# Second buffers, new PSUM banks, 96+96 contraction and a new order behind the experts of a five-stage transformer kernel

## The chip, the cores and the metric

The kernel runs on one core of one Trainium2 chip. The metric is the device time of one execution in microseconds; 2% of it is 7.3 us. One launch does all of the work, from the images to the output.

## The reference

Sixteen inputs of 96 tokens (64 image patches and 32 text rows), each token 192 wide, in float32:

```
h = tok(x);  h = concat([h, txt], axis=1)                 # 16 x 96 x 192
h = h + attn0(layernorm(h));  h = h + experts(layernorm(h))
# the part that is changed:
q, k, v = layernorm(h) @ w_qkv.T                          # 12 heads of 16
q = q / max(sum_n |q|, 1e-12);  k = k / max(sum_n |k|, 1e-12)
h = h + (q @ (k^T v)) @ w_proj.T + b_proj                 # linear attention
Xn = l2_normalize(layernorm(h));  sp = l2_normalize(slots) * scale
logits = Xn @ sp                                          # 96 tokens x 32 slots
D = softmax(logits, over tokens);  C = softmax(logits, over slots)
H = gelu((D^T Xn) @ W_down + b_down);  h = h + C @ (H @ W_up + b_up)
```

## The kernel before, in words

The 16 inputs are four groups `j` of four. A group has 384 tokens, held as `NB = 3` blocks of 128 rows; a block holds 32 tokens of each of its four inputs. `h[:, j, blk]` is the running sum. Each engine (TensorE `pe`, ScalarE `act`, VectorE `ve`, GpSimd `gp`, SyncE `sp`) has one program, written out by hand as a list of calls, and carries it out strictly in that order. Engines meet only at semaphores. `free(name=count)` in TensorE's list is a wait that protects a PSUM bank or a buffer; `need(...)` is one inside a helper.

The tokens, the first attention and the experts take the first 260 us and are not changed. Behind them TensorE first does `combine(j, part)`: the experts' rows of groups 0 and 1 are weighed and added into `h`; groups 2 and 3 get theirs by indirect DMAs that GpSimd issues (`fetch_row`) and VectorE adds (`add_rows`). Then comes, for each group, one round of the linear attention:

- VectorE `linear_moments`, GpSimd `norm_scale("b", ...)`, VectorE `linear_norm`: the layer norm, into `xn`.
- TensorE `turn_linear`: turns `xn` into PSUM; ScalarE `keep_linear_inputs` copies it to `xnT`.
- TensorE `linear_queries` and `linear_keys_values`; ScalarE copies to `q1T` and `kv1`. The 192 features are contracted as 128 + 64. `xnT[:, 0]` holds features 0 to 127; `xnT[:, 1]` holds the other 64 twice, in rows 0 to 63 and 64 to 127, so that two matmuls of 64 rows can run side by side in the two halves of the array.
- TensorE `key_products` (k^T v, L801) and `key_sums` (sum of |k|, L809; VectorE `key_norms` makes `abs_k` for it).
- VectorE `own_heads` masks the products into `kv_bd`; `query_norms`, `norm_products` and `scale_queries` scale `q1T`.
- TensorE `linear_outputs` (L820), ScalarE `keep_linear_outputs` to `o1T`, TensorE `linear_project` in two parts (L830), VectorE `add_linear`.

And one round of the soft mixture: VectorE `soft_moments`, GpSimd `soft_scale`, VectorE `soft_norm` into `xs`; TensorE `turn_soft`, ScalarE `keep_soft_inputs` to `xsT`; TensorE `soft_logits` (L850); VectorE `soft_max`, `token_shift`; ScalarE `exp_slots`, `exp_tokens`; VectorE `slot_weights` into `dsp_bd` and `token_weights`; TensorE `soft_inputs` (L858), ScalarE `keep_slots`. For all groups together: `soft_hidden` (groups 0 to 2, then 3, L866), `gelu_slots`, `keep_own`, then for each group `slot_outputs` (L873), `add_up_bias`, `token_outputs` (L882), `add_soft` and the stores.

The buffers `xn`, `o1T`, `xs`, `xsT`, `dsp_bd` and the small statistics exist once, so that for instance `linear_norm(j)` needs `turn_linear(j - 1)` to be over. PSUM has eight banks: 0 and 1 serve the turned inputs and the queries, 2 to 4 the keys and values, 1 to 4 the key products, 1 and 2 the outputs, 3 and 4 the projection, 5 to 7 the soft mixture. A copy out of a bank must be over before the next user writes it.

## Time and profile before

| | |
|---|---|
| time, median of 3 runs | 366.97 us (364.63 to 372.05) |
| the profiled execution | 366.12 us, its span 364.0 us |
| TensorE busy | 325.9 us, 90% of the span |
| VectorE / ScalarE / GpSimd busy | 195.5 / 112.1 / 52.1 us |
| first combine matmul | 259.81 us |
| end of the last matmul | 360.13 us |

The table is read so: TensorE is busy nine tenths of the time, but that is a mean over the program. In the 40 slices of the page it stands at 9 or more up to about 260 us and lower behind it. All that is changed lies between 259.81 and 360.13 us, 100.3 us long; behind it come one addition by VectorE and the last stores, 3.9 us. A TensorE duration in the rows includes the emptying of its pipeline; where steps follow one another without a wait, the step's price is from its start to the start of the next. The 9 to 48 instructions of one step stand in one row; a float32 matmul counts as two instructions.

### The profile page before, as it was taken

What the parts mean: (1) busy time and instruction counts of PE and PEld (TensorE: products, weight loads), DVE (VectorE), ACT (ScalarE), POOL (GpSimd) and SP (SyncE); (2) the same over time, 40 slices, a digit from 0 to 9 for tenths busy, and PEclk for the clock granted to TensorE, in tenths of its full rate; (3) what the DMA queues carried; (4) which work ended last, traced back from release to release, by engine and by line L of the source; (5) the groups of instructions that cost most, each with busy time, mean ns of one, the idle gap of its engine ahead of it and who ended that gap; (6) DMA issues with size and microseconds to landing.
All of it is one profiled execution on the core that took longest, in us unless ns stands there. A gap on an engine that the chain in (4) does not pass through costs nothing.

```text
span 364.0 us, 9315 instructions
## 1 busy us (share of the span) xinstructions
PE 325.9 (90%) x3978; PEld 216.6 (60%) x3978; DVE 195.5 (54%) x636; ACT 112.1 (31%) x218; POOL 52.1 (14%) x99
## 2 busy tenths in 40 slices
PE   4898999887788989999999999999987899997765
PEld 3675567655665337475656657475854556666455
DVE  2925497899999971142312111120367655968655
ACT  1224444665642431404041221203012213333140
POOL 8403222100011000000010000000087201100100
PEclk9999999999999999999999999999999989999889
DMA  7936011332030000504132240000012000000005
GB/s 266 346 85 220 2 38 31 117 125 96 19 105 1 2 0 2 151 17 137 50 103 74 81 137 16 23 2 22 24 54 67 13 0 0 3 2 2 0 0 130
DMA packets 15876, 23.29 MB, mean 64 GB/s; under 512 B 3770, under 2 KB 11932, under 8 KB 15836
## 3 DMA queue, kind: packets, MB, share of 16 engines
q1 hardware_dynamic: 14364, 20.93, 18.4%
q0 software_dynamic: 576, 1.18, 1.2%
q10 hardware_dynamic: 896, 0.59, 0.7%
q8 instruction: 31, 0.51, 0.6%
q14 instruction: 9, 0.07, 0.1%
HBM read 19.94 MB, written 2.75 MB: 62 GB/s over the span
## 4 chain that ended last, share of the span: by engine, by line
PE 61%; DVE 20%; SPq 7%; issue 4%; DMA 3%; POOL 2%; ACT 2%; DVEq 0%; POOLq 0%; ACTq 0%
PE banks L719 18%; PE banks L734 17%; SPq L320 4%; PE banks L496 3%; PE banks L249 3%; PE banks L778 2%; PE banks L858 2%; DVE sb_onehot_combT L1695 2%; PE banks L820 2%; PE banks L830 2%; PE banks L788 2%; DMA sb_tok_xeT<-in_xhalo 2%; DVE sb_stat L1517 1%; POOL sb_onehot_combT L455 1%; PE banks L782 1%
## 5 line engine op out<-in xcount | busy, mean ns | idle before, releaser
L719 PE MATMUL banks<-sb_tok_xeT,sb_wi_sl 128*128 128x480 f32 (+1 forms) x192 | 64.9, 590 | 1.1 <-ACT sb_tok_xeT L1236 1.1
L734 PE MATMUL banks<-sb_wo_sl,sb_attn_hidT_attn 128*60 128x192 f32 x768 | 64.1, 327 | 0.0
L734 PEld LDWEIGHTS banks<-sb_wo_sl,sb_attn_hidT_attn 128*60 128x60 f32 x768 | 52.9, 133 | 12.4 <-issue 4.0
L1251 ACT ACTIVATE sb_attn_hidT_attn<-banks 128x480 f32<-128x480 f32 x48 | 25.6, 569 | 95.7 <-PE banks L719 95.7
L719 PEld LDWEIGHTS banks<-sb_tok_xeT,sb_wi_sl 128*128 128x128 f32 (+1 forms) x192 | 24.9, 187 | 37.7 <-issue 35.8
L1743 DVE COPY sb_w_tok_e_out<-banks 60x384 f32<-60x384 f32 x16 | 8.9, 555 | 61.9 <-PE banks L734 61.6
L496 PE MATMUL banks<-sb_tok_xeT 128*32 128x193 f32 (+1 forms) x512 | 24.7, 328 | 1.5 <-DMA sb_tok_xeT<-in_xhalo 1.5
L496 PEld LDWEIGHTS banks<-sb_tok_xeT 128*32 128x32 f32 (+1 forms) x512 | 17.2, 109 | 7.2 <-issue 4.5
L1745 DVE COPY sb_onehot_combT<-banks 60x384 f32<-60x384 f32 x16 | 8.9, 555 | 22.1 <-PE banks L734 22.0
L618 PE MATMUL banks<-sb_w_v,sb_xrT 97*32 97x96 f32 x512 | 13.7, 249 | 1.8 <-issue 1.2
L1155 ACT ACTIVATE sb_onehot_combT<-sb_tok_xeT 128x1024 f32<-128x1024 f32 x8 | 8.5, 1058 | 19.3 <-DMA sb_tok_xeT<-in_xhalo 19.0
L1517 DVE BATCH_NORM_STATS2 sb_stat<-sb_h 128x6 f32<-128x192 f32 x48 | 14.1, 348 | 0.5
L858 PE MATMUL banks<-sb_attn_hidT_attn 128*96 128x128 f32 x48 | 8.8, 353 | 5.7 <-DVE sb_attn_hidT_attn L1865 5.7
L618 PEld LDWEIGHTS banks<-sb_w_v,sb_xrT 97*32 97x32 f32 x512 | 10.8, 110 | 5.2 <-issue 2.1
L455 POOL DMA_INDIRECT sb_onehot_combT<-expert_rows,sb_row_of x12 | 12.1, 1011 | 6.6 <-DMA expert_rows<-sb_onehot_combT 3.4
L508 PE MATMUL banks<-sb_w_tok_e_out,sb_ln_b 128*128 128x192 f32 x30 | 7.7, 421 | 5.2 <-DMA sb_w_tok_e_out<-in_wtok 5.2
L443 POOL TENSOR_TENSOR sb_soft_stat<-sb_soft_stat,sb_half 128x6 f32<-128x6 f32 x4 | 5.3, 1337 | 47.4 <-DVE sb_soft_stat L1832 47.4
L1730 DVE TENSOR_TENSOR sb_comb<-sb_cst,sb_slot_of 128x480 f32<-128x480 f32 x6 | 3.9, 654 | 15.0 <-PE banks L249 15.0
L778 PE MATMUL banks<-sb_w_kv,sb_xnT 128*128 128x384 f32 x24 | 9.9, 520 | 1.9 <-DVE sb_attn_hidT_attn L1815 1.6
L858 PEld LDWEIGHTS banks<-sb_attn_hidT_attn 128*96 128x96 f32 x48 | 7.7, 221 | 6.4 <-DVE sb_attn_hidT_attn L1865 6.4
L438 POOL MEMSET sb_attn_hidT_attn<- 1x384 f32 x1 | 0.4, 412 | 77.0 <-PE banks L734 77.0
L249 PE MATMUL banks<-sb_cst,sb_attn_hidT_attn 128*128 128x128 f32 (+1 forms) x72 | 10.4, 278 | 0.7 <-DVE sb_attn_hidT_attn L1577 0.7
(252 smaller groups left out, 537.6 us busy)
## 6 DMA issues: line engine op xcount, KB each, us to landing
sb_wo_sl<-in_wo SPq DMA_DIRECT2D x8, 576.0 KB, 4.5
sb_tok_xeT<-in_xin SPq DMA_DIRECT2D x8, 448.0 KB, 5.4
sb_wi_sl<-in_wi SPq DMA_DIRECT2D x8, 288.0 KB, 3.0
sb_wi_sl<-in_wi SPq DMA_DIRECT2D x24, 96.0 KB, 3.0
sb_w_tok_e_out<-in_wtok SPq DMA_DIRECT2D x2, 960.0 KB, 7.5
expert_rows<-sb_onehot_combT SPq DMA_DIRECT2D x8, 192.0 KB, 4.2
sb_w_tok_e_out<-in_wtok SPq DMA_DIRECT2D x1, 576.0 KB, 9.5
out<-sb_h SPq DMA_DIRECT2D x8, 72.0 KB, 2.0
```

The costliest lines, as they stand in the source:

```text
L249: return nc.tensor.transpose(dst, src, ident[0:rows, 0:rows])
L320: sp.dma_start(dst, src).then_inc(sem("attn0_in"), 16)
L455: gp.indirect_dma_start(rows_in[:, i], None, expert_rows, bass.IndirectOffsetOnAxis(ap=row_of[:, i:i + 1], axis=0)).then_inc(sem(f"rows_in ...
L496: nc.tensor.matmul(PS[QB * b:QB * b + QB, bank, at:at + D + 1], x_k[0:rows, (2 * j + b // 2) % NX, t, cols], w_eff[0:rows, t], start=(t == ...
L618: mm = nc.tensor.matmul(PS[32 * r:32 * r + 32, V_BANK[b % 2], s * C1:(s + 1) * C1], xrT[:, at:at + 32], w_v4[:, r], start=True, stop=True)
L719: mm = nc.tensor.matmul(PS[:, banks[z], 0:SLOTS], lhs, rhs.rearrange("k g c -> k (g c)"), start=first, stop=not first)
L734: mm = nc.tensor.matmul(PS[64 * z:64 * z + CAP, 4 + hf, pr * D:(pr + 1) * D], hidT[:, e % 2, f, g * CAP:(g + 1) * CAP], wo_sl[:, q, f], st ...
L778: nc.tensor.matmul(PS[:, 2 + blk, 0:2 * D], xnT[:, 0, blk * 128:(blk + 1) * 128], w_kv1[:, 0], start=True, stop=False)
L858: mm = nc.tensor.matmul(PS[0:HD, 7, dh * 128:(dh + 1) * 128], xs[:, blk, dh * HD:(dh + 1) * HD], dsp_bd[:, blk].rearrange("t q s -> t (q s ...
L1251: nc.scalar.activation(hidT[:, e % 2, f], PS[:, HID_BANKS[(e * (FT // 2) + f // 2) % 2][f % 2], 0:SLOTS], ACT.Relu).then_inc(sem("hidT"), 1)
L1517: ve.bn_stats(stat6[:, blk], h[:, j, blk]).then_inc(sem("stat6"), 1)
L1743: ve.tensor_copy(e_out[64 * (e % 2):64 * (e % 2) + CAP, z:z + 3:2, e // 2], src).then_inc(sem("e_out"), 1)
```

## The change

Behind the experts and nowhere else:

1. The 192 features are contracted as 96 + 96 in `linear_queries` and `linear_keys_values`; `turn_linear` then needs two turns for each block instead of three, and the weights arrive in two DMAs instead of eight.
2. Second buffers for `xn`, `o1T`, `xs`, `xsT` (the four inputs) and for `dsp_bd`, `mv_b`, `rs_b`, `mv_s`, `soft_st`; the waits in the helpers look one group further back.
3. PSUM banks assigned anew, by named constants.
4. A new order in the lists of all four engines. `linear_keys_values` is called for one block at a time.

The core of the diff:

```diff
-LAYER1_DMAS = 15
+LAYER1_DMAS = 9
+COMB_BANKS = ((0, 3), (3, 4))
+LIN_T_BANKS, LIN_Q_BANKS, LIN_KV_BANKS = (0, 1), (1, 3), (1, 0, 4)
+PROD_BANK, SUM_BANK, LIN_O_BANKS, PROJ_BANKS = 4, 0, (1, 2), (3, 2)
+SOFT_T_BANKS, SOFT_LOG_BANK, SOFT_IN_BANK, SOFT_HID_BANKS = (6, 4), 5, 2, (0, 1)
+SLOT_Y_BANKS, TOKEN_Y_BANKS = (6, 3), ((2, 6), (1, 0))
...
-        o1T = mid[0:HD + 1, 3264:4032].rearrange("k (a t) -> k a t", a=2)
+        o1T = [x.rearrange("k (a t) -> k a t", a=2) for x in (mid[0:HD + 1, 3264:4032], x_space[0:HD + 1, 5888:6656])]
+        xn_b = [xn[:], x_space[:, 3584:4160].rearrange("t (b d) -> t b d", b=NB)]
...
-            gp.memset(o1T[HD:HD + 1, 0], 1.0).then_inc(sem("pads_zero"), 1)
+            then(gp.memset(o1T[0][HD:HD + 1, 0], 1.0))
+            gp.memset(o1T[1][HD:HD + 1, 0], 1.0).then_inc(sem("pads_zero"), 1)
...
             def turn_linear(j):
-
                 for blk in range(NB):
                     pe.wait_ge(sem("b_xn"), NB * j + blk + 1)
-                    cols = slice(blk * 128, (blk + 1) * 128)
-                    flip(PS[:, 0, cols], xn[:, blk, 0:128])
-                    flip(PS[:, 1, cols], xn[:, blk, D - 128:D])
-                    mm = flip(PS[0:DT, 1, cols], xn[:, blk, 128:D])
+                    for kh in range(2):
+                        mm = flip(PS[0:HD, LIN_T_BANKS[kh], blk * 128:(blk + 1) * 128], xn_b[j % 2][:, blk, kh * HD:(kh + 1) * HD])
                 mm.then_inc(sem("b_xnT_ps"), 1)
-            def linear_keys_values(j, blks):
-
+            def linear_keys_values(j, blk):
                 pe.wait_ge(sem("b_xnT"), j + 1)
-                for blk in blks:
-                    nc.tensor.matmul(PS[:, 2 + blk, 0:2 * D], xnT[:, 0, blk * 128:(blk + 1) * 128], w_kv1[:, 0],
-                                     start=True, stop=False)
-                for blk in blks:
-                    rows = slice(blk % 2 * DT, (blk % 2 + 1) * DT)
-                    nc.tensor.matmul(PS[:, 2 + blk, 0:2 * D], xnT[rows, 1, blk * 128:(blk + 1) * 128], w_kv1[rows, 1],
-                                     start=False, stop=True).then_inc(sem("b_kv_ps"), 1)
+                for kh in range(2):
+                    mm = nc.tensor.matmul(PS[:, LIN_KV_BANKS[blk], 0:2 * D], xnT[:, kh, blk * 128:(blk + 1) * 128],
+                                          w_kv1[:, kh], start=(kh == 0), stop=(kh == 1))
+                mm.then_inc(sem("b_kv_ps"), 1)
             def linear_queries(j):
                 pe.wait_ge(sem("b_xnT"), j + 1)
                 for mh in range(2):
-                    nc.tensor.matmul(PS[0:HD, mh, 0:TOK], w_q1[:, 0, mh * HD:(mh + 1) * HD], xnT[:, 0], start=True, stop=False)
-                for mh in range(2):
-                    rows = slice(mh * DT, (mh + 1) * DT)
-                    mm = nc.tensor.matmul(PS[0:HD, mh, 0:TOK], w_q1[rows, 1, mh * HD:(mh + 1) * HD], xnT[rows, 1],
-                                          start=False, stop=True)
+                    for kh in range(2):
+                        mm = nc.tensor.matmul(PS[0:HD, LIN_Q_BANKS[mh], 0:TOK], w_q1[:, kh, mh * HD:(mh + 1) * HD], xnT[:, kh],
+                                              start=(kh == 0), stop=(kh == 1))
                 mm.then_inc(sem("b_q_ps"), 1)
...
             combine(0, 0)
             combine(0, 1)
+            free(moe_h=2)
             combine(1, 0)
...
-            free(b_kv=3, b_xnT=2)
+            free(b_kv=3)
             key_products(0)
+            free(b_xnT=2)
             key_sums(0)
...
             def linear_norm(j):
                 ve.wait_ge(sem("b_rs"), j + 1)
-                need(ve, "b_xnT_ps", j)
-                normalize("b_xn", j, xn, mv_b, rs_b)
+                need(ve, "b_xnT_ps", j - 1)
+                normalize("b_xn", j, xn_b[j % 2], mv_b[:, j % 2], rs_b[:, j % 2])
```

`keep_linear_outputs`, `keep_soft_inputs`, `soft_norm` and `slot_weights` change in the same way (`need(..., j)` becomes `need(..., j - 1)`).

What the new lists do is seen at three places. The first is on TensorE, between the key products of group 0 (L801, both kernels) and those of group 1. L809 is `key_sums`, L820 `linear_outputs`; keys and values are L778 and L782 before, L783 now, the queries L788 and L791 before, L791 now. Before:

```order
L801 MATMUL banks<-sb_attn_hidT_attn 96x96 x24
L809 MATMUL banks<-sb_qmask,sb_attn_hidT_attn 96x4 x2
L778 MATMUL banks<-sb_w_kv,sb_xnT 128x384 x2
L782 MATMUL banks<-sb_w_kv,sb_xnT 128x384 x2
L778 MATMUL banks<-sb_w_kv,sb_xnT 128x384
L782 MATMUL banks<-sb_w_kv,sb_xnT 128x384
L820 MATMUL banks<-sb_attn_hidT_attn 96x3x32 x8
L801 MATMUL banks<-sb_attn_hidT_attn 96x96 x24
```

Now:

```order
L801 MATMUL banks<-sb_attn_hidT_attn 96x96 x24
L809 MATMUL banks<-sb_qmask,sb_attn_hidT_attn 96x4 x2
L783 MATMUL banks<-sb_w_kv,sb_xnT 128x384 x4
L820 MATMUL banks<-sb_attn_hidT_attn 96x3x32 x8
L783 MATMUL banks<-sb_w_kv,sb_xnT 128x384 x2
L791 MATMUL banks<-sb_xnT,sb_w_q 96x384 x4
L801 MATMUL banks<-sb_attn_hidT_attn 96x96 x24
```

The outputs of group 0 have moved ahead of the third block of keys, and the queries of group 1 stand between those outputs and the key products, where ScalarE copies the outputs and the keys out.

The second is VectorE in the last soft mixture, up to the normalized input of group 3 (`soft_norm`, L1525 before, L1529 now; `slot_weights` ends with L1865 before, L1871 now; `token_weights` ends with L1877 and L1883; `add_linear` is L1821/L1824 and L1825/L1828). Before:

```order
L1865 TENSOR_TENSOR sb_attn_hidT_attn<-sb_attn_hidT_attn,sb_qmask 128x384
L1517 BN_STATS sb_stat<-sb_h 128x6 x3
L1521 BN_AGGR sb_mv_s<-sb_stat 128x2 x3
L1831 TENSOR_SCALAR sb_soft_stat<-sb_mv_s 128x3
L1832 TENSOR_SCALAR sb_soft_stat<-sb_mv_s 128x3
L1870 TENSOR_REDUCE sb_c_st<-sb_attn_hidT_attn 128x3
L1871 RECIPROCAL sb_c_st<-sb_c_st 128x3
L1872 TENSOR_TENSOR sb_attn_hidT_attn<-sb_attn_hidT_attn,sb_c_st 128x96
L1875 STREAM_TRANSPOSE sb_attn_hidT_attn<-sb_attn_hidT_attn 128x96
L1877 TENSOR_TENSOR sb_tok_xeT<-sb_attn_hidT_attn,sb_qmask 128x384
```

Now:

```order
L1876 TENSOR_REDUCE sb_c_st<-sb_attn_hidT_attn 128x3
L1877 RECIPROCAL sb_c_st<-sb_c_st 128x3
L1878 TENSOR_TENSOR sb_attn_hidT_attn<-sb_attn_hidT_attn,sb_c_st 128x96
L1881 STREAM_TRANSPOSE sb_attn_hidT_attn<-sb_attn_hidT_attn 128x96
L1883 TENSOR_TENSOR sb_tok_xeT<-sb_attn_hidT_attn,sb_qmask 128x384
L1855 TENSOR_REDUCE sb_d_st<-banks 128x1
L1856 STREAM_TRANSPOSE sb_attn_hidT_attn<-banks 128x96
L1858 TENSOR_REDUCE sb_c_st<-sb_attn_hidT_attn 128x3
L1861 TENSOR_TENSOR sb_attn_hidT_attn<-sb_attn_hidT_attn,sb_c_st 128x96
```

Before, the weights of group 2 are ready ahead of the moments of group 3; now the token weights of group 1 and the soft maximum of group 2 stand between the moments and the norm of group 3, and `slot_weights(2)` comes behind that norm.

The third is GpSimd behind the experts: row fetches (L455 before, L464 now) and the norm scales of groups 0 and 1. Before:

```order
L455 DMA sb_onehot_combT<-expert_rows,sb_row_of 128x192 x2
L358 TENSOR_SCALAR sb_p_var<-sb_mv_b 128x3
L360 TENSOR_TENSOR sb_rs_b<-sb_p_var,sb_half 128x3
L455 DMA sb_onehot_combT<-expert_rows,sb_row_of 128x192 x3
L358 TENSOR_SCALAR sb_p_var<-sb_mv_b 128x3
L360 TENSOR_TENSOR sb_rs_b<-sb_p_var,sb_half 128x3
L455 DMA sb_onehot_combT<-expert_rows,sb_row_of 128x192 x7
```

Now:

```order
L464 DMA sb_onehot_combT<-expert_rows,sb_row_of 128x192 x2
L365 TENSOR_SCALAR sb_p_var<-sb_mv_b 128x3
L367 TENSOR_TENSOR sb_rs_b<-sb_p_var,sb_half 128x3
L464 DMA sb_onehot_combT<-expert_rows,sb_row_of 128x192 x4
L365 TENSOR_SCALAR sb_p_var<-sb_mv_b 128x3
L367 TENSOR_TENSOR sb_rs_b<-sb_p_var,sb_half 128x3
L464 DMA sb_onehot_combT<-expert_rows,sb_row_of 128x192 x3
```

The scale of group 1 has moved behind one more fetch, that of group 2 ahead of three.

## Rows read from the trace of the kernel before

**Rows 1.** Stretch, length, busy PE, PEld, DVE, ACT, POOL (count), then PEclk, DMA, GB/s.

```profile
328.28:348.87 20.59, 13.60 (x105) 10.37 (x105) 14.98 (x60) 5.75 (x15) 1.39 (x2) 0.90 0.00 1
...
259.81:360.13 100.32, 85.06 (x728) 60.20 (x722) 67.28 (x233) 25.36 (x53) 22.45 (x25) 0.95 0.07 20
```

**Rows 2.** TensorE's waits from 259.81 to 360.13 us, the longest of them.

```profile
PE banks L858 <- DVE sb_attn_hidT_attn L1865: 5.7, 3, 2.4
PE banks L801 <- issue: 1.9, 2, 0.9
```

**Rows 3.** Timeline of TensorE: start, length, what, and idle time before.

```profile
290.34 2.87 PE L788 MATMUL banks<-sb_xnT,sb_w_q 128*96 128x384 f32 x4 [0.63 <-DVE sb_attn_hidT_attn L1815]
...
304.21 1.53 PE L788 MATMUL banks<-sb_xnT,sb_w_q 128*96 128x384 f32 x4 [0.43 <-ACT sb_attn_hidT_attn L1279]
...
306.49 1.57 PE L830 MATMUL banks<-sb_w_proj,sb_attn_hidT_attn 97*128 97x192 f32 x8
307.90 1.15 PE L249 MATMUL banks<-sb_cst,sb_xn 128*128 128x128 f32 x9
308.88 0.82 PE L830 MATMUL banks<-sb_w_proj,sb_attn_hidT_attn 97*128 97x192 f32 x4
309.54 0.82 PE L249 MATMUL banks<-sb_cst,sb_attn_hidT_attn 128*96 128x128 f32 x6
310.28 1.27 PE L801 MATMUL banks<-sb_attn_hidT_attn 32*96 32x96 f32 x48
311.49 0.54 PE L850 MATMUL banks<-sb_attn_hidT_attn,sb_slot_n 96*32 96x96 f32 x16
312.63 1.56 PE L778 MATMUL banks<-sb_w_kv,sb_xnT 128*128 128x384 f32 x4 [0.61 <-DVE sb_attn_hidT_attn L1815]
314.12 0.92 PE L782 MATMUL banks<-sb_w_kv,sb_xnT 64*128 64x384 f32 x4
314.97 0.91 PE L778 MATMUL banks<-sb_w_kv,sb_xnT 128*128 128x384 f32 x2
...
316.65 1.60 PE L820 MATMUL banks<-sb_attn_hidT_attn 96*96 96x96 f32 x16
318.08 1.48 PE L858 MATMUL banks<-sb_attn_hidT_attn 128*96 128x128 f32 x12
319.40 1.45 PE L788 MATMUL banks<-sb_xnT,sb_w_q 128*96 128x384 f32 x4
...
338.01 2.88 PE L858 MATMUL banks<-sb_attn_hidT_attn 128*96 128x128 f32 x12 [1.94 <-DVE sb_attn_hidT_attn L1865]
341.35 2.86 PE L866 MATMUL banks<-sb_tok_xeT,sb_w_down 96*96 96x384 f32 x8 [0.46 <-ACT sb_tok_xeT L1300]
344.04 0.82 PE L249 MATMUL banks<-sb_cst,sb_attn_hidT_attn 128*96 128x128 f32 x6
```

**Rows 4.** Timeline of VectorE, 334 to 342 us, columns as above.

```profile
334.93 0.55 DVE L1821 TENSOR_TENSOR sb_h<-sb_h,banks 128x384 f32<-128x384 f32 x1
335.39 0.25 DVE L1849 TENSOR_REDUCE sb_d_st<-banks 128x1 f32<-128x96 f32 x1
...
336.33 0.35 DVE L1824 TENSOR_TENSOR sb_h<-sb_h,banks 128x192 f32<-128x192 f32 x1
336.59 0.16 DVE L1860 RECIPROCAL sb_d_st<-sb_d_st 128x1 f32<-128x1 f32 x1
...
337.88 0.87 DVE L1517 BATCH_NORM_STATS2 sb_stat<-sb_h 128x6 f32<-128x192 f32 x3
...
339.15 0.24 DVE L1870 TENSOR_REDUCE sb_c_st<-sb_attn_hidT_attn 128x3 f32<-128x96 f32 x1
...
340.72 0.16 DVE L1836 TENSOR_TENSOR sb_soft_stat<-sb_mv_s,sb_soft_stat 128x3 f32<-128x3 f32 x1
...
341.72 0.96 DVE L1525 TENSOR_SCALAR sb_attn_hidT_attn<-sb_h,sb_mv_s,sb_soft_stat 128x192 f32<-128x192 f32 x3
```

**Rows 5.** The chain that ended last: landing of a row fetch of group 2.

```profile
273.01 4.02 DMA sb_onehot_combT<-expert_rows,sb_row_of
```

More of the change, by code:

```diff
@@ L1116, in _ @@
-            free(s_xtT=2)
-            turn_soft(2)
-            linear_project(3, 0)
-            free(b_knorm=4)
-            soft_logits(2)
-            linear_project(3, 1)
+            free(b_kv=12, s_dexp=1, s_lgT=1)
+            key_products(3)
+            key_sums(3)
+            free(b_q1T=4)
+            linear_project(2, 0)
+            linear_project(2, 1)
+            free(b_kvbd=4)
+            turn_soft(1)
+            free(b_h=6)
+            soft_inputs(0)
+            soft_logits(1)
```

307 lines of the change are left out of this document (153 added, 154 removed).

## The prediction

> **What bounds the kernel now.** I read the busy time by stretch first. The changed part is 100.3 us long, of which TensorE is busy 85.1, so it stands idle 15.3 us; its mean granted clock is 0.95 [rows 1]. It is worst near the end: 13.6 us busy in 20.6, clock 0.90 [rows 1]. So TensorE's work bounds most of this part and its waits bound the rest. The table of waits names two kinds. 5.7 us stand before `soft_inputs` (L858) in three waits for VectorE's `dsp_bd` [rows 2]. 1.9 us stand before `key_products` (L801) as "issue" [rows 2]: no semaphore event explains them there, but the list has `free(b_xnT=2)` and `free(b_o1T=1)` in front of these two steps, and ScalarE's copies end just as the steps begin, so they are bank conflicts: banks 1 to 4 can't be written while ScalarE copies out of 0 to 2. The other 7.7 us are a dozen waits of up to 1 us, each a product that VectorE or ScalarE has just made.
>
> The timeline adds the clock. `soft_inputs` at 338.01 us takes 2.88 us after a wait of 1.94; the same step at 318.08 takes 1.48 at full clock. The first two query matmuls take 2.87 at 290.34 and 1.53 at 304.21 [rows 3]. These two stretches at 1.2 GHz instead of 2.4 cost 1.4 and 1.3 us. A mean clock of 0.95 over 100.3 us [rows 1] means some 10 us at half clock, which can cost no more than 5.0; I take 4.3. So the 100.3 us are 15.3 idle, 4.3 for the clock and 80.7 of work at full clock.
>
> The sum below gives new values for these three.
>
> **Work: contraction by 96+96.** Turning one group costs 0.98 us for nine instructions (307.90 to 308.88) and 0.74 for the six of `turn_soft`, the form that the new `turn_linear` has (309.54 to 310.28) [rows 3]. Four groups: 4 x -0.24 = -1.0 us. The queries cost 2.28 us before (304.21 to 306.49). Now they are four matmuls with 96 rows and 384 columns, the form of L866, which costs 2.69 (341.35 to 344.04): 4 x 0.41 = +1.6 us. Keys and values cost 4.02 us a group (312.63 to 316.65). Now they are six matmuls of that size. At the 0.64 us apiece that L866 comes to within its row they would cost 3.8; at the 1.49 of two matmuls with a change of shape behind them (312.63 to 314.12), three times, 4.5 [rows 3]. I take 4.25, since most blocks now stand alone between other steps: +0.9, with ends at -0.7 and +1.8. Together the work grows by 1.5 us (0 to 2.4), to 82.2.
>
> What packing is worth can be read too: the two 64-row matmuls side by side cost 0.85 us (314.12 to 314.97), where one full one costs about 0.65 [rows 3]. So the packing saves less than one matmul in two. The Trainium skill, "TensorEngine Tiling (Array Packing)", section "Theoretical Speedup", gives row tiling at 64 rows or fewer up to 2x, which speaks against this change: by it each pair given up would cost a full 0.65 us, 5.2 us over the eight pairs where the rows make it 2.5. Its section "Tiling Modes" also says that a change of mode drains the engine; with that the 0.85 of the trace agrees.
>
> **Work that is moved costs nothing in itself.** The GpSimd memset of the second `o1T` is 1 x 384 and runs while GpSimd waits for the experts' rows. Two DMAs instead of eight on SyncE's queue fall into the experts, where no matmul waits for weights. All prices of VectorE and ScalarE stay; the copy of `xnT` is 96 rows high instead of 128 but as long.
>
> **Idle: what goes.** I followed the new lists on all engines with the durations of the trace, from the first combine on. Rounds 0 to 3 of the attention now have other TensorE work wherever a product is being made: the third block of keys and the queries stand between `linear_outputs` and `key_products`, the turn of the next group behind them, so ScalarE's 0.8 us copies and VectorE's masks are covered. The cover is thick, 2.7 us of queries for a 0.8 us copy. The bank waits of 1.9 us go, since `key_products` now writes 4 to 7 and the turn 0 and 1. Up to `linear_outputs(3)` only these remain: 0.35 for the new `free(moe_h=2)` (VectorE's addition, with `combine(1, 0)` and everything of TensorE behind it), 0.9 for the first copy of `xnT`, before which TensorE has nothing, and 0.9 in three small ones before `key_sums(0)`, `linear_outputs(0)` and `linear_outputs(3)`, for VectorE.
>
> **Idle: what is late next.** From `linear_outputs(3)` on VectorE has more to do than TensorE. It starts when `scale_queries(3)` ends, and until the first block of `soft_norm(3)` VectorE carries out, by the starts in [rows 4]: `soft_max` with `token_shift` 0.94 (335.39 to 336.33), `soft_norm(2)` 1.9 (1.00 from 340.72 to 341.72, and three blocks), `slot_weights(1)` 1.29, `add_linear(3)` 0.46 + 0.26, `soft_moments(3)` 1.27, `token_weights(1)` 1.57, `soft_max(2)` 0.94, and the first 1.3 of `soft_norm(3)`: 9.9 us. TensorE has there `linear_outputs` 1.43, `linear_project` 1.41 + 0.66, one `turn_soft` 0.74, one `soft_inputs` 1.32, one `soft_logits` 0.5: 6.1 us [rows 3]. So it idles 3.9 us, of which some 3 in one piece before `turn_soft(3)`. Then `soft_inputs(2)` needs the rest of the norm and `slot_weights(2)`, 0.6 + 1.3 = 1.9 us, against 0.74 for `turn_soft(3)`: 1.15 us. Behind that `soft_hidden` (2.69) covers `slot_weights(3)`, which before was the wait of over 2 us, and only 0.6 for the Gelu before the last part is left.
>
> Sum of the waits: 0.35 + 0.9 + 0.9 + 3.9 + 1.15 + 0.6 = 7.8 us, from the end of a step's price. A busy row runs about 0.16 longer than the price (1.48 against 1.32 at 318.08 [rows 3]), so in the profile's way of counting some 9 stops take 1.3 off: 6.5 us idle instead of 15.3, a gain of 8.8.
>
> **Clock.** The stretches at 290 and 349 us should stay at full clock, since the waits ahead of them go; the 3 us wait before `turn_soft(3)` is longer than the 1.94 that preceded the fall at 338.01, so I leave one fall there, on `soft_inputs(2)`, 1.4 us. Gain 4.3 - 1.4 = 2.9. The Trainium skill, "TensorE: Matmul & The Clock Gate", section "Why this matters for your kernels", says that TensorE's clock halves over idle gaps between bursts and that bursts should follow closely; with the falls in these rows the trace agrees, and the forecast has one for the same reason.
>
> **Row fetches.** `fetch_row(2, 2, 1)` now comes ahead of `norm_scale("b", 1)`, which ends some 1.3 us later. `turn_linear(1)` waits for that norm but comes 1.5 us later still. The other price is the landing: one such fetch took 4.0 us from its start [rows 5]. If it does so again, `add_rows(2, 2)` and VectorE's queue behind it (`query_norms(0)`, `key_norms(0)`, `scale_queries(0)`) start 0.8 later, and `linear_outputs(0)` with them. I take half, 0.4, with ends 0 and 0.8.
>
> **The sum.** 8.8 + 2.9 - 1.5 - 0.4 = 9.8 us. The part shrinks from 100.3 to 90.5, the span from 364.0 to about 354.2 and the profiled execution from 366.12 to 356.3. The median stands 0.85 above the profiled execution, so the forecast is 366.97 - 9.8 = 357.2 us.
>
> **The rivals.**
>
> *More falls of the clock.* The waits of the attention rounds are small in my count, but each is a difference of two long sums; if two more stretches run at 1.2 GHz, at 1.4 to 1.6 us each, the time is 360.2. For it: a wait of only 0.63 us stands before the fall at 290.34. Against it: between the rounds almost nothing waits any more. Chance 0.15.
>
> *Dearer attention.* Keys at 4.5 us a group (+0.9), the fetch late (+0.4) and the small waits twice as long (+2.1): 360.6. For it: the new list changes shape at nearly every step. Chance 0.12.
>
> *Cheaper end.* No fall of the clock, no late fetch, keys back to back (-1.6): 357.2 - 1.4 - 0.4 - 1.6 = 353.8. Chance 0.12.
>
> *Slower: VectorE becomes the chain of every round.* Its queue is strict, and in a round `own_heads`, `norm_products` and `scale_queries`, 2.5 us together, lie between `key_products` and `linear_outputs`, behind whatever stands ahead of them in VectorE's list. If an addition or a norm there waits for a TensorE step that stands behind `linear_outputs` in time, the two engines take turns: 2.5 us for the chain and up to 1.6 for the clock, 4.1 a round. From two and a half exposed rounds on the gain is gone; all four give 357.2 + 16.4 = 373.6. VectorE's busy share, 67.3 of 100.3 us [rows 1], speaks against it: it has room outside the last stage. Chance 0.05.
>
> **How the numbers follow.** The forecast (355 to 359.5) has 0.56. 2% is 7.3 us, about what a measurement of this kernel can tell from no change: a time under 359.6 is faster. The forecast and the cheaper end lie below it (0.68), of the two dearer rivals some 0.09 as well: faster 0.77, same 0.18, slower 0.05. The range goes from the cheaper end's 353.8 to 361.5, which takes in both dearer rivals.
>
> **What would show it.** Right: no wait before L801; `linear_outputs` of group 3 starts some 9 us earlier than before (about 321.5); a wait of about 3 us before the turn of group 3, ended by VectorE's L1529; `soft_inputs` takes 1.48 three times and 2.88 once; queries 2.7 and keys about 4.2 us a group. Wrong: waits of over 0.5 us in the rounds ended by `scale_queries` or by the copies, more than one row of `soft_inputs` or queries at double length, or idle time of VectorE between 309 and 333 us, where I have it always at work.

## The result, and the profile after

The changed kernel took 355.88 us (median of four executions, 351.79 to 359.15) beside 365.8 for the kernel before in the same comparison. The ratio is 0.967, with a 95% interval of 0.960 to 0.973: faster by 3.3%. The forecast of 357.2 has the sign right. The ratio leaves disturbed executions out, in which the clock is lower: of the changed kernel 351.79 and 354.5 stay, 353.1 on average and 0.7 us below the range, and of the kernel before three, 365.2 on average.

The profiled execution took 351.79 us, with a span of 350.0. These are the stretches of the changed part, columns as in [rows 1]:

```profile
257.43:267.90 10.47, 8.98 (x106) 7.29 (x101) 5.60 (x18) 0.80 (x1) 6.23 (x8) 1.00 0.15 47
267.90:317.52 49.62, 49.16 (x446) 34.73 (x447) 40.26 (x138) 16.28 (x30) 15.10 (x18) 1.00 0.07 19
317.52:346.24 28.72, 23.65 (x164) 19.84 (x164) 21.48 (x80) 8.70 (x22) 1.89 (x2) 0.88 0.08 21
257.43:346.24 88.81, 81.79 (x716) 61.86 (x710) 67.34 (x233) 25.77 (x53) 23.22 (x26) 0.96 0.08 23
```

The part is 88.8 us long instead of 100.3 [rows 1]. From the first keys to `linear_outputs(3)` TensorE is busy 49.2 of 49.6 us at full clock: the rounds of the attention have no waits left. All the idle time lies at the two ends: 1.5 us ahead of the first keys, and 5.5 from the wait before `linear_outputs(3)` on. The table of TensorE's waits is now short, where the one before had 18 of them, among them those of [rows 2]:

```profile
PE banks L257 <- DVE sb_tok_xeT L1529: 3.2, 1, 3.2
PE banks L783 <- ACT sb_xnT L1266: 1.0, 1, 1.0
PE banks L830 <- ACT sb_tok_xeT L1283: 0.9, 1, 0.9
PE banks L866 <- ACT sb_tok_xeT L1304: 0.5, 1, 0.5
PE banks L767 <- DVE sb_h L1760: 0.5, 1, 0.5
PE banks L858 <- DVE sb_attn_hidT_attn L1871: 0.4, 1, 0.4
PE banks L820 <- DVE sb_attn_hidT_attn L1813: 0.4, 1, 0.4
```

TensorE's timeline answers to [rows 3]; first one of the rounds, then the end:

```profile
267.90 2.82 PE L783 MATMUL banks<-sb_w_kv,sb_xnT 96*128 96x384 f32 x8 [1.03 <-ACT sb_xnT L1266]
270.56 2.74 PE L791 MATMUL banks<-sb_xnT,sb_w_q 96*96 96x384 f32 x8
273.13 1.45 PE L783 MATMUL banks<-sb_w_kv,sb_xnT 96*128 96x384 f32 x4
274.43 0.82 PE L257 MATMUL banks<-sb_cst,sb_tok_xeT 128*96 128x128 f32 x6
275.25 1.27 PE L801 MATMUL banks<-sb_attn_hidT_attn 32*96 32x96 f32 x48
...
317.52 1.57 PE L820 MATMUL banks<-sb_attn_hidT_attn 96*96 96x96 f32 x16 [0.41 <-DVE sb_attn_hidT_attn L1813]
319.98 2.23 PE L830 MATMUL banks<-sb_w_proj,sb_tok_xeT 97*128 97x192 f32 x12 [0.88 <-ACT sb_tok_xeT L1283]
...
324.13 0.54 PE L850 MATMUL banks<-sb_attn_hidT_attn,sb_slot_n 96*32 96x96 f32 x16
327.86 1.51 PE L257 MATMUL banks<-sb_cst,sb_tok_xeT 128*96 128x128 f32 x6 [3.20 <-DVE sb_tok_xeT L1529]
329.81 2.84 PE L858 MATMUL banks<-sb_attn_hidT_attn 128*96 128x128 f32 x12 [0.44 <-DVE sb_attn_hidT_attn L1871]
332.59 0.87 PE L850 MATMUL banks<-sb_tok_xeT,sb_slot_n 96*32 96x96 f32 x16
333.39 3.23 PE L866 MATMUL banks<-sb_tok_xeT,sb_w_down 96*96 96x384 f32 x8
336.45 1.48 PE L858 MATMUL banks<-sb_tok_xeT 128*96 128x128 f32 x12
```

`key_products` (L801) starts with no wait. A pair of blocks of keys costs 2.66 us (267.90 to 270.56), a block alone 1.30 (273.13 to 274.43). At the end one wait of 3.20 us stands before the turn of group 3, and the four rows behind it are longer than at full clock: 1.51 instead of 0.82, 2.84 instead of 1.48, 0.87 instead of 0.54, 3.23 instead of 2.86: 2.75 us. VectorE, beside [rows 4], is without a gap up to that turn and then waits for TensorE:

```profile
326.25 0.26 DVE L1861 TENSOR_TENSOR sb_attn_hidT_attn<-sb_attn_hidT_attn,sb_c_st 128x96 f32<-128x96 f32 x1
...
327.43 0.96 DVE L1529 TENSOR_SCALAR sb_tok_xeT<-sb_h,sb_mv_s,sb_soft_stat 128x192 f32<-128x192 f32 x3
...
333.52 0.26 DVE L1855 TENSOR_REDUCE sb_d_st<-banks 128x1 f32<-128x96 f32 x1 [2.29 <-PE banks L850]
```

Work at full clock is 81.79 - 2.75 = 79.0 us. So 11.5 us of the part went as 8.2 of idle time (15.3 to 7.0), 1.6 of clock (4.3 to 2.75) and 1.7 of work (80.7 to 79.0). By estimate the 1.7 us of work are how a row is counted, not cheaper steps: a row ahead of a wait runs on past its price, and 11 such waits are gone (see below). The other 2.4 us of the 14 between the profiles lie ahead of the part: its first combine starts at 257.43 instead of 259.81.

### The profile page after: what moved, and what is told of

Its sections match the earlier page's. It is cut to its first block, busy times and chain, and to the rows that moved or that the text cites. A ratio compares the mean times of both kernels' runs of the same rounds, so it can differ in the third digit from the quotient of the medians.

```text
span 350.0 us, 9283 instructions
## 1 busy us (share of the span) xinstructions
PE 322.4 (92%) x3966; PEld 217.4 (62%) x3966; DVE 194.9 (56%) x636; ACT 112.4 (32%) x218; POOL 53.1 (15%) x100
## 3 DMA queue, kind: packets, MB, share of 16 engines
HBM read 19.80 MB, written 2.75 MB: 64 GB/s over the span
## 4 chain that ended last, share of the span: by engine, by line
PE 72%; DVE 21%; issue 2%; DMA 2%; ACT 2%; SPq 0%; DVEq 0%; ACTq 0%
PE banks L728 18%; PE banks L743 18%; PE banks L505 6%; PE banks L783 5%; PE banks L791 3%; PE banks L257 3%; PE banks L767 2%; DVE sb_onehot_combT L1699 2%; DMA sb_w_tok_e_out<-in_wtok 2%; PE banks L830 2%; PE banks L820 2%; DVE sb_stat L1521 2%; DVE sb_tok_xeT L1480 1%; DVE sb_attn_hidT_attn L1581 1%; DVE sb_smax L1569 1%
## 5 line engine op out<-in xcount | busy, mean ns | idle before, releaser
L1255 ACT ACTIVATE sb_attn_hidT_attn<-banks 128x480 f32<-128x480 f32 x48 | 25.7, 569 | 95.7 <-PE banks L728 95.7
L1749 DVE COPY sb_onehot_combT<-banks 60x384 f32<-60x384 f32 x16 | 8.9, 555 | 22.1 <-PE banks L743 22.0
L783 PE MATMUL banks<-sb_w_kv,sb_xnT 96*128 96x384 f32 x48 | 17.6, 497 | 1.0 <-ACT sb_xnT L1266 1.0
L627 PEld LDWEIGHTS banks<-sb_w_v,sb_xrT 97*32 97x32 f32 x512 | 10.8, 109 | 5.1 <-issue 2.1
L464 POOL DMA_INDIRECT sb_onehot_combT<-expert_rows,sb_row_of x12 | 12.3, 1026 | 6.0 <-issue 3.0
L783 PEld LDWEIGHTS banks<-sb_w_kv,sb_xnT 96*128 96x128 f32 x48 | 8.5, 190 | 5.4 <-ACT sb_xnT L1266 1.3
L791 PE MATMUL banks<-sb_xnT,sb_w_q 96*96 96x384 f32 x32 | 11.0, 486 | 0.0
L690 PE MATMUL banks<-sb_onehot_combT,sb_xn 64*128 64x480 f32 x48 | 10.7, 578 | 0.2 <-issue 0.2
```

The source lines that it names most:

```text
L464: gp.indirect_dma_start(rows_in[:, i], None, expert_rows, bass.IndirectOffsetOnAxis(ap=row_of[:, i:i + 1], axis=0)).then_inc(sem(f"rows_in ...
L627: mm = nc.tensor.matmul(PS[32 * r:32 * r + 32, V_BANK[b % 2], s * C1:(s + 1) * C1], xrT[:, at:at + 32], w_v4[:, r], start=True, stop=True)
L690: mm = nc.tensor.matmul(PS[:, banks[hf], 0:E * CAP], xn2[rows, j, blk, 0:128], onehot[rows, j % 2, blk], start=(blk == 0), stop=(blk == NB ...
L783: mm = nc.tensor.matmul(PS[:, LIN_KV_BANKS[blk], 0:2 * D], xnT[:, kh, blk * 128:(blk + 1) * 128], w_kv1[:, kh], start=(kh == 0), stop=(kh ...
L791: mm = nc.tensor.matmul(PS[0:HD, LIN_Q_BANKS[mh], 0:TOK], w_q1[:, kh, mh * HD:(mh + 1) * HD], xnT[:, kh], start=(kh == 0), stop=(kh == 1))
L1255: nc.scalar.activation(hidT[:, e % 2, f], PS[:, HID_BANKS[(e * (FT // 2) + f // 2) % 2][f % 2], 0:SLOTS], ACT.Relu).then_inc(sem("hidT"), 1)
```

## The experiments

There were fifteen runs, one of them (e5) of the changed kernel itself, each with the kernel before beside it. Ratios are to that one, with their 95% intervals. "Part" is the stretch from the first combine to the end of the last matmul in the profile; its idle time is the length less TensorE's busy time.

### One part of the change in the old kernel

**e1**: only the second buffers (`xn_b`, `o1T`, `xs`, `xsT`, `dsp_bd` and the statistics, with their waits), old order.

```diff
-                need(ve, "b_xnT_ps", j)
-                normalize("b_xn", j, xn, mv_b, rs_b)
+                need(ve, "b_xnT_ps", j - 1)
+                normalize("b_xn", j, xn_b[j % 2], mv_b[:, j % 2], rs_b[:, j % 2])
```

> The kernel before with the second buffers alone (xn, o1T, xs, xsT, dsp_bd and the statistics), old banks, old contraction, old order. Theory A (the order carries the gain, the buffers only permit it): in the old order almost no wait is for a buffer, VectorE stood 0.7 us before the norm of group 1 for soft_inputs(0) and that is all; the part from the first combine to the last matmul stays at 99 to 100.3 us, no change that can be told. Theory B (the engines were held up by single buffers): half of the gain or more, the part at 95 us or less, the time 5 us or more below the kernel before.

Measured 1.004 (0.998 to 1.010); idle time in the part 15.8 us against 15.3, 2.1 of them in the gaps that the last section shows. The length of the part, 108.8 us, can't be held against the expected one, since the mean granted clock was 0.87 in it. The buffers alone give nothing.

**e2**: only the contraction by 96+96, old order.

```diff
-                for blk in blks:
-                    nc.tensor.matmul(PS[:, 2 + blk, 0:2 * D], xnT[:, 0, ...], w_kv1[:, 0], start=True, stop=False)
-                for blk in blks:
-                    rows = slice(blk % 2 * DT, (blk % 2 + 1) * DT)
-                    nc.tensor.matmul(PS[:, 2 + blk, 0:2 * D], xnT[rows, 1, ...], w_kv1[rows, 1], start=False, stop=True)
+                for blk in blks:
+                    for kh in range(2):
+                        nc.tensor.matmul(PS[:, 2 + blk, 0:2 * D], xnT[:, kh, ...], w_kv1[:, kh], start=(kh == 0), ...)
```

> The kernel before with the contraction 96+96 alone (turns, keys and values, queries, their weights), old banks, buffers and order, keys still called in two parts. Theory A (contraction neutral): queries 2.65 instead of 2.28 us a group, turns 0.72 instead of 0.98, keys 4.0 as before; the part grows by 0 to 0.6 us, to 100.3 to 100.9. Theory C (giving up the changes of shape is the gain): keys fall below 3.7 us a group and the part by 2 us or more.

Measured 0.997 (0.992 to 1.003). A group of keys is 3.95 us there (301.20 to 305.15) against 4.02 [rows 3]. Nothing in the time. The part of its profile is 103.3 us, longer than either theory has it, with the gaps and the fall of the clock that the last section shows. One of its ten executions took 1810 us and the others 366 to 375; the ratio is without it, and why it was so long is not known.

**e9**: e1 and e2 together; only banks and order stay old.

> The kernel before with the second buffers of e1 and the 96+96 of e2 together, old banks and old order. It leaves only the banks and the order out of the change. Theory A: as each alone, nothing; ratio to before 0.99 to 1.01, key_products still idle 0.9 us in two rounds, over 5 us of waits before soft_inputs. Rival: the parts work together, and most of the 3.3% is here without any new order: 0.975 or less.

Measured 0.997 (0.992 to 1.001), idle time 16.6 us (the part is 108.6 us, at a mean clock of 0.87). So the new banks and order are needed for all of the gain. No run has the new order with all of the old banks, so how the gain divides between the two is open.

### One part of the change taken back in the new kernel

**e3**: the changed kernel with 128+64. Its 64-row matmuls of the keys never run side by side; those of the queries still do.

> The changed kernel with the contraction 128+64 back, one block of keys at a time as in its order, so that the 64-row matmuls of keys have no partner. Theory A: a lone block costs two steps of 0.85 instead of one of 1.32, 5.1 us a group instead of 4.0; queries fall from 2.65 to 2.28, turns rise from 0.71 to 0.98: +4.4 - 1.5 + 1.1 = about +4 us on the changed kernel's part of 88.8, so 92 to 93. Theory D (the contraction doesn't matter in the new order either, since VectorE is the bound): 88.8 to 89.8.

Measured 0.987 (0.975 to 1.000), median 364.7. Here are two blocks, one after the other:

```profile
278.66 0.89 PE L789 MATMUL banks<-sb_w_kv,sb_xnT 128*128 128x384 f32 x2
279.48 0.91 PE L791 MATMUL banks<-sb_w_kv,sb_xnT 64*128 64x384 f32 x2
281.76 1.65 PE L789 MATMUL banks<-sb_w_kv,sb_xnT 128*128 128x384 f32 x2 [1.38 <-DVE sb_den L1812]
283.34 1.65 PE L791 MATMUL banks<-sb_w_kv,sb_xnT 64*128 64x384 f32 x2
```

At full clock, in the first two rows, the half with 64 rows takes as long as the one with 128, 0.82 to 0.84 us, with nothing beside it. A block comes to about 1.65 us instead of 1.35, and with what the changes of shape cost the steps beside it a group of keys is 1.0 us dearer (from `key_sums(1)` to `soft_logits(1)`, 30.26 us in e3 and 28.80 in the changed kernel, with two groups of keys and of queries and one linear turn). Over four groups that is 3.9 us, less 1.6 for the cheaper queries, plus 1.4 for the turns: some 3.7, near the 4 that were expected. The part is 100.6 us and not 92 to 93, because 1.4 us of wait stand before the third row and the clock is at half from 281 to 295 us. Why VectorE was late there was not looked for. The Trainium skill, "TensorEngine Tiling (Array Packing)", section "Theoretical Speedup", gives up to 2x at 64 rows, and the trace agrees: two of them side by side took 0.85 us in the kernel before ([rows 3], 314.12 to 314.97), one alone takes 0.84. But that needs a pair, and e3 has none among the keys. In two places of the new order (267.90 and 276.91 us in the changed kernel) two blocks follow each other and could be packed (in the second, `free(b_knorm=1)` stands between them). A packed pair cost 2.34 us before ([rows 3], 312.63 to 314.97) and two blocks cost 3.33 in e3 (268.25 to 271.58), so by estimate 2.0 of the 3.7 us would come back. That kernel was not run.

**e7**: the waits that the old banks would force, in the new order.

```diff
             key_sums(0)
+            free(b_kvbd=1)
             linear_keys_values(1, 0)
...
             key_sums(1)
+            free(b_kvbd=2)
             linear_keys_values(2, 0)
```

> The changed kernel with free(b_kvbd=1) ahead of linear_keys_values(1, 0) and free(b_kvbd=2) ahead of linear_keys_values(2, 0). These are the waits that the old banks would force: keys in 2 to 4 can't be written before VectorE has masked the products out of 1 to 4. It prices the banks within the new order. Theory A: in the first profile the mask of group 0 ends at 278.6 us and these keys start at 276.9, so 1.8 us of idle time come in round 0, and 0.1 in round 1 (288.74 against 288.61); up to 1.4 more if the clock falls on the keys behind it. Most of it is lost for good: the part is 1.5 to 3.2 us longer. Rival: the 3.2 us wait before the turn of group 3 takes it up, since VectorE sets the end: under 0.5.

The wait in round 0 is there, 1.6 us, and none in round 1. Behind it the keys of the profiled execution run at half clock, 5.45 us instead of 2.83, and its part is 100.1 us at a mean clock of 0.88, so it can't be compared with the expected 1.5 to 3.2 us more. The ratio is 0.963 (0.955 to 0.972), no worse than the changed kernel's. So the banks hold 1.6 us of idle time that the profile shows; that it costs time was not shown, the clock's own spread being larger.

**e8**: single `xn`, `o1T`, `mv_b`, `rs_b`; the buffers of the soft mixture stay double.

> The changed kernel with one xn, one o1T, one mv_b and one rs_b instead of two each; xs, xsT, dsp_bd and the statistics of the soft mixture stay double, since the new order writes the norm of a group before soft_inputs has read the one before it. Theory A: only one use of these second buffers shows in the first profile: VectorE's linear_norm(3) at 285.8 us would wait for turn_linear(2), which ends at 287.0. That delays scale_queries(1) by 1.2 us to 292.0, 0.1 us later than linear_outputs(1) starts now. The time stays within 0.5 us: these second buffers are worth nothing. Rival: the delay runs through VectorE's queue (the norm, the queries' sums, the mask of group 1) to the end: 1 to 1.5 us slower, more with a fall of the clock.

Measured 0.961 (0.953 to 0.969), idle time 7.4 us. One wait of 0.24 us before `linear_outputs(1)` is new, ended by VectorE. These second buffers are worth nothing that the times can show in this order.

**e6**: the old combine banks, without `free(moe_h=2)`.

> The changed kernel with the old banks of the combine, (6, 7) and (5, 4), and without free(moe_h=2). Theory A: the wait of 0.45 us in front of combine(1, 0) goes, the rounds behind it begin 0.4 us earlier, and VectorE's chain at the end starts earlier by as much: the part from the first combine on is 0.3 to 0.5 us shorter, not measurable in the times. Rival: key_products, now writing 4 to 7, has to wait for the additions out of these banks, or the end takes the gain back as a longer wait before the turn of group 3: 0.

The wait before `combine(1, 0)` is gone, but idle time is 7.4 us and the ratio 0.962 (0.956 to 0.968): nothing that can be measured, and the expected 0.4 us can't be told in one profile, since its clock fell once more, at 322 us.

**e5**: the changed kernel again.

> The changed kernel once more, as a control for the profile and for the other kernels of this job. Theory A: its part from the first combine to the last matmul is again 88 to 89 us, with one wait of about 3 us before the turn of group 3 and half clock behind it, and what differs from the first profile is the start of the first combine, which has no part in the change: 257.4 to 259.8 us in the six profiles so far. Then the median is 353 to 356. Rival: the start at 257.43 came from the change (two DMAs instead of eight on SyncE's queue); then it is at 257.4 again, and every kernel with 96+96 has it.

The part is 88.79 us and the clock falls in the same place, but the part starts at 257.08. The median was 357.8 (351.5 to 361.7), ratio 0.971. Over all seventeen profiles the start lies between 257.1 and 261.1 us: old DMA list 259.8, 258.2, 257.4, 257.5; new one 257.1 to 261.1. So the rival (two DMAs instead of eight) falls: the 2.4 us are no effect of the change. The traces show two things that they go with. The profile of before, and no other, has a wait of TensorE for a DMA of the inputs:

```profile
33.59 2.96 PE L496 MATMUL banks<-sb_tok_xeT 128*32 128x193 f32 x64 [1.51 <-DMA sb_tok_xeT<-in_xhalo]
```

It was already 0.7 us late ahead of that wait and stayed some 2.3 us late behind it. And between 70 and 113 us the clock was at half for 10.2 us in e7 (first combine at 261.13), for 6.8 us in e4, e6, e8 and e15 (258.70 to 259.63) and nowhere in the two profiles of the changed kernel (257.43 and 257.08).

### The waits and the clock at the end

**e4**: the changed kernel with five dummy matmuls (128 x 384, into bank 7) in the 3.2 us wait before `turn_soft(3)`.

```diff
             soft_logits(2)
+            idle_work(5)
             turn_soft(3)
```

> The changed kernel with five extra 128x384 matmuls into the unused bank 7 between soft_logits(2) and turn_soft(3), where TensorE waited 3.2 us for VectorE; their result is used by nobody. Theory A (TensorE's idle time brings the clock down there, and that costs 2.8 us of doubled steps, of which 0.7 is hidden by VectorE): turn_soft(3) 0.8, soft_inputs(2) 1.5, soft_logits(3) 0.5, soft_hidden 2.9 us; the part at 86.8 to 87.3 instead of 88.8. Rival E (the clock falls there for another reason, or the doubled steps are hidden behind VectorE anyway): the part stays at 88.5 to 89.2.

```profile
327.33 3.49 PE L838 MATMUL banks<-sb_cst 128*128 128x384 f32 x10
330.66 0.93 PE L257 MATMUL banks<-sb_cst,sb_tok_xeT 128*96 128x128 f32 x6
332.54 1.52 PE L862 MATMUL banks<-sb_attn_hidT_attn 128*96 128x128 f32 x12 [0.95 <-DVE sb_attn_hidT_attn L1876]
```

The clock stays at full speed, and `soft_inputs(2)` takes 1.52 us. The part is 87.4 us, 0.1 above what theory A gave and well below the rival's 88.5, though it holds a wait of 0.41 us before `key_sums(0)` that the changed kernel's profile doesn't have. Ratio 0.959 (0.950 to 0.969), median 352.8. Of the 2.75 us that the fall cost, 0.5 come back as a longer wait for VectorE (0.95 instead of 0.44). From `soft_logits(2)` to the end it is 20.2 us instead of 22.1.

**e10**: e4 with four dummies, and the last mask of `token_weights` of groups 0 to 2 on GpSimd.

```diff
                 ve.transpose(cmbT ...).then_inc(sem("s_cmbT"), 1)
+                if j < 3:
+                    return
...
+                gp.wait_ge(sem("s_cmbT"), j + 1)
+                gp.tensor_tensor(cmb_bd[:, j], cmbT ..., qmask ..., ALU.mult).then_inc(sem("s_cmbbd"), 1)
```

> The changed kernel with dummy matmuls before turn_soft(3) as in e4 (four instead of five), and with the last step of token_weights for groups 0 to 2 (the multiplication by the mask, 0.56 us each, that makes cmb_bd) on GpSimd instead of VectorE. Theory A: VectorE sets the end from 301 us on, where it has hardly a gap. Two of these steps lie in that stretch, 0.47 us apart in its queue each: the first block of the norm of group 3, and soft_inputs(2) with it, come 0.5 to 0.9 us earlier, and the part is 86.5 to 87.0 us instead of the 87.4 of e4. Rival: the small gaps that VectorE has before exp and norm take it up, or GpSimd slows VectorE down: 87.2 to 88.

The part is 87.3 us: the rival. Of the two masks that leave VectorE's queue in the stretch, the one at 309 us brought nothing by `linear_outputs(3)`, which starts 60.7 us behind the first combine, in e4 60.6. What the other gained was lost again. VectorE and GpSimd of e10 in the same microsecond, from their timelines:

```profile
326.08 0.25 DVE L1873 TENSOR_REDUCE sb_c_st<-sb_attn_hidT_attn 128x3 f32<-128x96 f32 x1
326.37 0.68 DVE L1876 TENSOR_TENSOR sb_attn_hidT_attn<-sb_attn_hidT_attn,sb_c_st 128x96 f32<-128x96 f32 x1
326.97 0.15 DVE L1856 TENSOR_TENSOR sb_soft_stat<-sb_mv_s,sb_soft_stat 128x3 f32<-128x3 f32 x1
```

```profile
326.11 0.83 POOL L457 TENSOR_TENSOR sb_tok_xeT<-sb_attn_hidT_attn,sb_qmask 128x384 f32<-128x384 f32 x1
```

The second row is the subtraction of `token_shift(2)`. In the changed kernel it takes 0.26 us (at 326.25, above). With GpSimd's multiplication beside it, which lasts to 326.94, it takes 0.68. The 0.42 us are nearly the 0.47 that had been moved. The Trainium skill, "SBUF — State Buffer", section "SBUF: two separate sides", says that a VectorE operation with two SBUF inputs and a GpSimd operation that reads SBUF lock each other out; the trace agrees: the subtraction ends 0.11 us behind the multiplication, at 327.05, and the reduction ahead of it, which has one input, keeps its 0.25 us. Even so this was the steadiest kernel: 350.3 to 352.4, median 350.6, ratio 0.951 (0.944 to 0.957). What made it so was not shown.

**e11**: VectorE's norm of group 3 first.

```diff
 VectorE:
+            soft_norm(3)
             soft_max(2)
             token_shift(2)
-            soft_norm(3)
 TensorE:
             soft_logits(2)
+            idle_work(3)
             turn_soft(3)
+            idle_work(2)
             free(s_xtT=2)
-            soft_inputs(2)
             free(s_dexp=3, s_lgT=3)
             soft_logits(3)
+            soft_inputs(2)
```

> The changed kernel with VectorE's soft_norm(3) ahead of soft_max(2) and token_shift(2), on TensorE soft_logits(3) ahead of soft_inputs(2), and dummy matmuls in the two gaps (three before turn_soft(3), two behind). It is another order with the same work on VectorE. Theory A: turn_soft(3) comes 0.95 us earlier, but slot_weights(2), behind all of these steps in either order, ends at the same time, so soft_inputs(2) starts where it did; only soft_logits(3), 0.5 us, is out of its way behind it: the part is 86.9 to 87.4 us against the 87.4 of e4. Rival: the wait before turn_soft(3) is what costs, and the whole 0.95 us is gained: 86.4.

The part is 89.5 us, outside both, because the clock fell at 321 us: `linear_project(3)` took 4.21 us instead of 2.23, after waits of 0.41 and 0.88. Ratio 0.952 (0.943 to 0.962). Inconclusive for its question.

**e12**: e10, e11 and e6 together.

> e10 and e11 together (two dummy matmuls before turn_soft(3), one behind), with the old combine banks and no free(moe_h=2) as in e6. Theory A: 0.4 us from the banks, 0.5 to 0.9 from the masks, up to 0.5 from the order: part 85.6 to 86.5 us, no clock fall, profiled execution some 350 us, median 351 to 353 against 355.9 of the changed kernel. Rival: with fewer dummy matmuls the remaining gaps let the clock fall, 2.5 to 4 us: 88 to 90 us.

Part 89.4 us, with the same fall (3.90 us), median 352.4, ratio 0.953 (0.944 to 0.962). No better than its parts. The length is the rival's, but not by the rival's cause: the fall came ahead of the gaps with few dummies. Two of its six executions took 361.9 and 364.1 us.

**e14** and **e15**: e4 (with four dummies) and e11, each with one more dummy in the 0.9 us wait before `linear_project(3, 0)`.

> The changed kernel with one dummy matmul in the 0.9 us wait before linear_project(3, 0) and four before turn_soft(3). Theory A: the falls at 321 us that e6, e11 and e12 had come from the 0.4 and 0.9 us waits around linear_outputs(3); with the second filled no profile shows one, the part is 87.2 to 87.6 us, and all executions lie within 1.5 us of each other, median 351 to 352 (e4: 350.9 to 355.6). Rival: they come from elsewhere: the executions spread as in e4, over 4 us.

> e11 (VectorE's soft_norm(3) first, soft_logits(3) ahead of soft_inputs(2), dummies in the gaps) with one more dummy matmul in the wait before linear_project(3, 0). Theory A: without the fall at 320 us, which made the part 89.5 us in e11, it is 86.9 us: 0.5 less than e4, since soft_logits(3) no longer stands behind soft_inputs(2). Median 350 to 351. Rival: the fall is there again, 89 us and more.

```profile
258.67:346.26 87.59, 82.73 (x726) 61.44 (x720) 67.50 (x233) 25.74 (x53) 23.20 (x26) 1.00 0.09 23
```

```profile
258.70:346.71 88.01, 83.39 (x728) 61.77 (x722) 67.58 (x233) 25.42 (x53) 23.34 (x26) 1.00 0.09 23
```

```profile
332.20 1.55 PE L862 MATMUL banks<-sb_attn_hidT_attn 128*96 128x128 f32 x12
334.30 2.79 PE L870 MATMUL banks<-sb_tok_xeT,sb_w_down 96*96 96x384 f32 x8 [0.55 <-ACT sb_tok_xeT L1311]
```

Neither profile has a fall (the first fence is e14's stretch, the others are e15's, with two rows of its timeline). That the 0.9 us wait starts it fits, but isn't settled: e14's executions still spread over 4.3 us (350.0 to 354.3), as e4's did, and one of e15's took 357.3 us. e15's part is 88.0 and not 86.9. The expectation had overlooked that `soft_logits(3)` behind `soft_inputs(2)` covers ScalarE's copy; taken away from there, it leaves 0.55 us before `soft_hidden`. In its new place it waits 0.36 us for ScalarE itself, and `soft_inputs(2)` starts 0.24 us later than in e14, both counted from `linear_outputs(3)`. So this order is no better than e14's. Ratios 0.962 (0.956 to 0.968) and 0.960 (0.954 to 0.965).

**e13**: the kernel before with dummies in eight of its waits, nothing else changed.

> The kernel before with dummy matmuls (128 x 384, into a bank that is out of use) in eight of its waits: one each before the waits for b_xnT=2, b_kvbd=1, b_o1T=1 and b_kvbd=2 (0.6 to 0.95 us long), two before soft_inputs(1) (1.3), three before soft_inputs(2) (1.9), one before soft_logits(3) (1.0) and three before soft_inputs(3) (2.4). Order, banks, buffers and contraction stay. Theory A: the clock stays at full speed in the part, which is then 96 to 97 us instead of 100.3 (4.3 us of clock gone, up to 1 us lost to dummies that end late); ratio to before 0.98 to 0.99. The rest of the changed kernel's gain, some 7 us, is idle time and work, which only the new order and banks take away. Rival: the clock is most of the gain: ratio 0.97 or less, as the changed kernel.

```profile
257.46:353.18 95.72, 89.42 (x754) 61.31 (x748) 67.45 (x233) 25.37 (x53) 22.69 (x25) 1.00 0.08 21
```

The part is 95.7 us at full clock, ratio 0.984 (0.978 to 0.990), executions within 3.6 us. Without its 13 dummies of 0.65 us its work is 81.0, near the 80.7 of the forecast. So full clock alone is worth 1.6% (1.0 to 2.2) to the old kernel, about half of the changed kernel's 3.3%. That doesn't make the clock half of what the changed kernel gained: in the two profiles it is 1.6 of the 11.5 us, and the idle time 8.2.

## Where the prediction was right, and which step failed

**Right: the mechanism and where it stops.** No wait before L801; the rounds full; a wait of 3.2 us before the turn of group 3, ended by L1529 (forecast 3); one fall of the clock behind it; `linear_outputs(3)` starts 10.8 us earlier counted from the first combine (forecast 9). The idle time is 7.0 us (forecast 6.5), in part because errors cancel: two of the three small waits did not come (0.41 us in all instead of 0.9), and the one before `soft_inputs(2)` was 0.44 us and not 1.15, since the turn ahead of it ran at half clock. That VectorE sets the end is shown by e4: with TensorE at full clock, the wait before `soft_inputs(2)` is 0.95, the forecast's 1.15 less the running-on of a row.

**The work was put 3.2 us too high: 82.2 against 79.0.** This is the largest mis-sized term of the sum. Queries came to 2.68 us (forecast 2.69) and turns to 0.71 (0.74). Keys came to 4.06 us a group (16.25 for the four: 3.96, 4.12, 3.98, 4.19) and not 4.25, since a block alone cost 1.29 to 1.47 us, little more than half a pair: 0.75 us of the 3.2. The rest is the running-on of a row ahead of a wait. I took it off the idle time that would be left, but left it in the work of the old kernel: 18 waits before and 7 after, at 0.16, are 1.8 us. (Its own nine stops at 0.16 are 1.4 and not 1.3.) That makes 2.6; 0.6 us are unaccounted. Counted from start to start, the new contraction cost some 0.7 us and not 1.5: queries 1.6 and keys 0.2 more, turns 1.1 less.

**The clock cost 2.75 us and not 1.4.** The fall took in four steps, not only `soft_inputs(2)`. Not all of the error is lost time: part of it ran while VectorE was the later engine anyway, 0.5 us by e4. By the same rows the fall cost 3.0 us in e8's profile, and with a second one 6.3 in e6's.

**The late row fetch was 0 in this profile, and real.** e14 shows it, where a fetch holds VectorE, and `key_sums(0)` (L809) waits 0.8 us for it:

```profile
274.58 0.88 DVE L1772 SCALAR_TENSOR_TENSOR sb_h<-sb_onehot_combT,sb_gate_row,sb_h 128x192 f32<-128x192 f32 x2 [0.65 <-DMA sb_onehot_combT<-expert_rows,sb_row_of]
```

Waits before L809 of 0.4 to 0.9 us stand in five of the profiles of the new order (e4, e7, e10, e14, e15), the forecast's 0 to 0.8; the 4.0 us landing of [rows 5] is the same kind of event.

**The part and the front.** The forecast had 90.5 us for the part and took the front from one profile. The part came to 88.8, and the front was 2.4 us shorter, which the range didn't hold: its ends were worked out from the changed part alone, so what lies ahead of it stood at nothing, without a reason given. With 1.7 and 2.4 us (and 0.1 behind the last matmul) the profiled execution came to 350.0 instead of 354.2 of span.

**So two steps failed together.** The work was mis-sized, 82.2 for 79.0, of which the clock took 1.35 us and the idle time 0.5 back, while the 0.4 for the row fetch was not spent; and the front was taken as fixed at 259.81, where it measured 257.43 here and 257.1 to 261.1 over all profiles. Either alone would have left the profiled execution inside the range (356.3 - 1.7 = 354.6, 356.3 - 2.4 = 353.9); both together took it out. The base adds to it: the forecast started from 366.97, and in the ratio the kernel before stands at 365.2, which is 1.8 of the 4.1 us between 357.2 and 353.1. The miss is small beside the scatter: a gain of 9.8 us is a ratio of 0.973, at the edge of the measured 0.960 to 0.973 and inside e5's 0.964 to 0.977. A range around a sum over one part needs the spread of what lies outside it.

**The rivals.** The cheaper end (353.8) is nearest, but for another reason: its dear half, no fall of the clock, did not happen in the profile, and e4 shows what it would have given. "More falls" is what the spread of the changed kernel's executions points to (351.5 to 361.7 in e5, with mean granted clocks of 0.990 down to 0.962), though only the profiled ones show where the clock fell. "Dearer attention" and "VectorE in every round" did not happen: waits in the rounds are 0.

**What each part is worth.** New banks and order: without them nothing is gained (e9). 96+96: nothing in the old order (e2), some 3.7 us of work in the new against an unpacked 128+64 (e3), and by estimate less than 2 against one that packs where two blocks follow each other. Second buffers: `xn` and `o1T` nothing that shows (e8); those of the soft mixture make the order possible, since `soft_norm(j + 1)` is now written before `soft_inputs(j)` has read.
